# Gates computed as rows, cell products alternating between row halves, and value products of two key tiles in one run

## The reference

```python
# 1. the cell: q is the normalized x, k and v are the context; 4 heads of 64
igate, fgate = concat(q,k,v) @ ig_kernel + ig_bias, concat(q,k,v) @ fg_kernel + fg_bias   # 4 + 4 numbers a token
F = cumsum(log_sigmoid(fgate)); D = exp(F_s - F_t + igate_t - max)       # lower triangle, 512 x 512 a head
h = (q k^T / 8 * D) / normalizer @ v ; x = x + headnorm(h)
# 2. attention: 2 experts x 16 heads of 16 channels, on n1 = layernorm(x)
scores = q k^T / 4 ; attn = softmax(scores) ; ctx = attn @ v              # 32 heads, 512 x 512 each
x = x + sum over experts of (ctx @ wo + bo) * router
# 3. feed-forward: the best 2 of 8 experts of the batch, 256 -> 512 (gelu) -> 256
```

## Time and profile before

| | us |
|---|---|
| median of 3 runs (1590.46 to 1594.23) | 1592.3 |
| the profiled execution | 1590.36 |
| its span | 1588.7 |
| PE busy | 1455.0 (92%) |
| DVE busy | 1107.6 (70%) |
| ACT busy | 924.9 (58%) |
| POOL busy | 357.3 (22%) |
| mean granted TensorE clock | 0.954 |

### The profile page before, as it was taken

One profiled execution on the slowest core, in us unless ns is written; L12 is line 12 of the kernel. 1 busy time (PEld: TensorE's weight loads), 2 busy tenths in 40 slices (PEclk: granted clock), 3 DMA queues, 4 the chain that ended last, 5 costly groups with the idle time before them and its releaser, 6 DMA issues. The chain is left out here.

```text
span 1588.7 us, 22385 instructions
## 1 busy us (share of the span) xinstructions
PE 1455.0 (92%) x7724; PEld 733.8 (46%) x7724; DVE 1107.6 (70%) x2305; ACT 924.9 (58%) x1696; POOL 357.3 (22%) x342
## 2 busy tenths in 40 slices
PE   4358989999999999999999999999999999999977
PEld 4324433545445544545435444455435454444434
DVE  5537796787668866787568876788667876776531
ACT  1114756475666675575665765666664766657651
POOL 3321133122121223122131232212231221320100
PEclk9568989999999999999999999999999999999998
DMA  4064306431254306431163404532064211542001
GB/s 117 0 76 71 68 2 80 68 68 54 35 95 69 58 27 92 70 66 43 34 100 41 94 27 53 95 61 53 22 93 67 68 43 33 74 60 61 15 14 67
DMA packets 93793, 92.68 MB, mean 58 GB/s; under 512 B 16593, under 2 KB 88401, under 8 KB 92657
## 3 DMA queue, kind: packets, MB, share of 16 engines
q1 hardware_dynamic: 93680, 91.25, 33.1%
HBM read 36.10 MB, written 4.26 MB: 25 GB/s over the span
## 5 line engine op out<-in xcount | busy, mean ns | idle before, releaser
L1160 ACT ACTIVATE prob<-psum 128x512 f32<-128x512 f32 x1024 | 566.7, 601 | 332.7 <-PE psum L551 328.3
L945 DVE TENSOR_REDUCE mx<-psum 128x1 f32<-128x512 f32 x1024 | 645.0, 682 | 134.7 <-PE psum L536 133.9
L551 PE MATMUL psum<-qst,kst 98*128 98x512 bf16 x1024 | 358.2, 388 | 13.7 <-ACT cxT L1153 8.1
L536 PE MATMUL psum<-kst,qst 96*128 96x512 bf16 x1024 | 321.6, 392 | 25.9 <-issue 12.2
L566 PE MATMUL psum<-prob,vst 128*17 128x512 f32 x2048 | 274.9, 609 | 0.4 <-ACT prob L1160 0.2
L551 PEld LDWEIGHTS psum<-qst,kst 98*128 98x128 bf16 x1024 | 97.0, 100 | 261.9 <-issue 172.6
L536 PEld LDWEIGHTS psum<-kst,qst 96*128 96x128 bf16 x1024 | 101.0, 100 | 136.9 <-issue 25.2
L1262 POOL CAST parts<-resid 128x512 bf16<-128x512 f32 x64 | 39.5, 617 | 476.0 <-DVE resid L868 475.9
L526 PE MATMUL psum<-w,cxT 128*128 128x256 f32 x512 | 119.5, 380 | 5.2 <-ACT cxT L1153 5.2
L510 PE MATMUL psum<-n2T,x 128*128 128x512 f32 x256 | 117.5, 598 | 5.4 <-DMA x<-in_L_ffn_fw 5.4
L526 PEld LDWEIGHTS psum<-w,cxT 128*128 128x128 f32 x512 | 96.4, 190 | 25.4 <-issue 10.0
(11 more groups left out here) (176 smaller groups left out, 1733.1 us busy)
## 6 DMA issues: line engine op xcount, KB each, us to landing
kst<-parts SPq DMA_DIRECT2D x192, 128.0 KB, 4.5
qst<-parts SPq DMA_DIRECT2D x192, 128.0 KB, 5.4
cmat<-G_dram SPq DMA_DIRECT2D x8, 1024.0 KB, 4.9
x<-in_L_ffn_fw SPq DMA_DIRECT2D x16, 512.0 KB, 3.3
w<-in_L_ffn_fw SPq DMA_DIRECT2D x16, 512.0 KB, 3.9
kin<-in_ctx SPq DMA_DIRECT2D x8, 512.0 KB, 3.7
xbuf<-in_x SPq DMA_DIRECT2D x8, 512.0 KB, 4.6
out<-acc SPq DMA_DIRECT2D x8, 512.0 KB, 3.7
```

What stands on the lines that cost most here:

```text
L536: e.matmul(psum[:, u.bank, :], qst[0:KROWS, h, t * P:(t + 1) * P], kst[0:KROWS, h, :], start=True, stop=True).then_inc(u.full, 1)
L551: e.matmul(psum[:, u.bank, :], kst[0:KROWS + 2, h, g * P:(g + 1) * P], qst[0:KROWS + 2, h, :], start=True, stop=True).then_inc(u.full, 1)
L945: e.tensor_reduce(mx[:, qq * QUAD + j, t:t + 1], psum[:, u.bank, :], AX, ALU.max).then_inc(u.free, 1)
L1160: e.activation(prob[:, g % 2, j, :], psum[:, u.bank, :], ACT.Exp).then_inc(u.free, 1)
```

## The change

1. **Gates as rows.** The gate weights become the stationary operand, padded to 36 columns (forget gates at 0 to 3, input gates at 32 to 35), and the transposed tokens (512 wide) the moving one: 4 matmuls give both gates as rows. The copy by DVE and the 8 transposes are gone. The input gates come out at partitions 32 to 35, so a DMA moves them to 0 to 3 (`gi_moved`).
2. **Cell products alternate** between the row halves: two heads are taken together, block by block (`cd0`, `cd1` instead of `cd0` to `cd3`), into two banks; the cross products likewise.
3. **Value products of two key tiles in one run.** In the second slot of every other tile (slot % 8 == 1) stand the products of the two tiles before, 8 matmuls in one run: 128 runs.
4. **All slot tables and `AHEAD` are new.** Gelu pieces of ScalarE stand between exponentials in 7 places of a batch instead of 5; the program holds 116 ACT_TABLE_LOADs instead of 88.

```diff
-        wgate = sb("wgate", [P, 3 * KC, 2, NH])
-        wgkv = sb("wgkv", [P, KC, 2, NH])
-        gbias = sb("gbias", [NH, 2])
+        GI = 32
+        wgate = sb("wgate", [P, 2 * KC, GI + NH])
+        gbias = sb("gbias", [GI + NH, 1])
...
+        gi_made = cmat[GI:GI + NH, 0, :]
...
-        CARRY, MADE = QUAD - 1, 121
-        VALUES, COPY, TURN = 3, 3, 15
-        LATER, SENT = 1, 1
+        CARRY, MADE = QUAD - 1, 126
+        VALUES, COPY, TURN = 1, 5, 15
+        LATER, SENT = 1, 5
...
-                for t in range(NT):
-                    for c in range(2 * KC):
-                        src = (kT if c < KC else qT)[:, c % KC, t * P:(t + 1) * P]
-                        w_ = (wgkv if c < KC else wgate)[:, c % KC].rearrange("p g h -> p (g h)")
-                        ins = e.matmul(psum[:, u.bank, t * 2 * NH:(t + 1) * 2 * NH], src, w_, start=c == 0,
-                                       stop=c == 2 * KC - 1)
+                for c in range(2 * KC):
+                    src = (kT if c < KC else qT)[:, c % KC, :]
+                    ins = e.matmul(psum[0:GI + NH, u.bank, :], wgate[:, c, :], src, start=c == 0, stop=c == 2 * KC - 1)
                 ins.then_inc(u.full, 1)
-                gates = u
-
-                for g in (1, 0):
-                    yield f"grow{g}"
-                    u = take("grow", b, g)
-                    e.wait_ge(gates.free, gates.n)
-                    for t in range(NT):
-                        o = (t * 2 + g) * NH
-                        ins = transpose(psum[0:NH, u.bank, t * P:(t + 1) * P], gcol[:, o:o + NH], P)
-                    ins.then_inc(u.full, 1)
...
-                for h in range(NH):
-                    yield f"cd{h}"
-                    u = take("cd", b, h)
-                    o = DH * (h % 2)
+                for hp in range(NH // 2):
+                    yield f"cd{hp}"
+                    us = []
                     for c in range(NT):
-                        s_ = slice(c * P, (c + 1) * P)
-                        ins = e.matmul(psum[:, u.bank, s_], kT[o:o + DH, h // 2, s_], qT[o:o + DH, h // 2, s_],
-                                       start=True, stop=True)
-                    ins.then_inc(u.full, 1)
+                        for par in range(2):
+                            if c == 0:
+                                us.append(take("cd", b, 2 * hp + par))
+                            s_, half = slice(c * P, (c + 1) * P), slice(DH * par, DH * (par + 1))
+                            ins = e.matmul(psum[:, us[par].bank, s_], kT[half, hp, s_], qT[half, hp, s_], start=True,
+                                           stop=True)
...
-                            if j == VALUES:
-                                if g > 0:
-                                    values(b, qq, g - 1)
-                                elif qq > 0:
-                                    values(b, qq - 1, NT - 1)
+                            if slot >= 2 * QUAD and slot % (2 * QUAD) == VALUES:
+                                for n in (slot // QUAD // 2 * 2 - 2, slot // QUAD // 2 * 2 - 1):
+                                    values(b, n // NT, n % NT)
...
+                values(b, NQ - 1, NT - 2)
                 values(b, NQ - 1, NT - 1)
...
-                yield "gates"
-                u = uses["gates", b]
-                e.wait_ge(u.full, u.n)
-                e.tensor_copy(gcol, psum[:, u.bank, 0:2 * NG]).then_inc(u.free, 1)
...
+                yield "grow1"
+                u = uses["gates", b]
+                e.wait_ge(u.full, u.n)
+                e.activation(gf, psum[0:NH, u.bank, :], ACT.Identity, bias=gbias[0:NH, :]).then_inc(aa.here("gf"), 1)
+                yield "grow0"
+                e.activation(gi_made, psum[GI:GI + NH, u.bank, :], ACT.Identity, bias=gbias[GI:GI + NH, :]).then_inc(u.free, 1)
...
+                yield "gi"
+                u = uses["gates", b]
+                e.wait_ge(u.free, u.n)
+                e.dma_start(gi, gi_made).then_inc(gi_moved, 16)
```

More of the change, by code:

```diff
@@ L258, in build @@
[L258 to L269, removed]
+        CARRY, MADE = QUAD - 1, 126
+        VALUES, COPY, TURN = 1, 5, 15
+        LATER, SENT = 1, 5
+        PE_A = slots(4, "kT0:6 kT1:0 qT0:0 qT1:2 gates:15 cols:13 cd0 cd1:2 st0:0 st1:0 st2 num0:10 num1:5 num2 "
+                     "num3:24 n1T0:0 n1T1:3 p0:7 p1 p2:6 p3:2 pv0:24 pv1:0 logits")
@@ new lines, in build @@
+        ACT_S = slots(6, "p4:0 p5:16 p6:0 p7:9 v0:4 v1")
+        POOL_A = slots(-1, "pw:23 vcopy:13 mask0:2 mask1 mask2:25 mask3:0 vw:0 hw:13 hs:8 hn x2:29 r1:4 r5:2 s0:0 s1:0 "
+                       "s2:5 s3")
+        POOL_C = slots(30, "acc0:9 r1")
+        POOL_S = slots(13, "s4 s5:2 s6:21 s7")
+        SP_A = slots(4, "ctx:0 x:19 gi G:84 s0:0 s1:15 s2:0 s3")
+        SP_C = slots(53, "w10:10 w20:5 w11:0 w21:20 out")
+        SP_S = slots(9, "s4:0 s5:30 s6:0 s7")
+        AHEAD = ("2232001002134332000100400120220011223110000000101022111100411041"
+                 "0021014411101101102103121002020102110012030210020020120101000000")
@@ L424, in stage_a @@
                     ins.then_inc(u.full, 1)
-                    for par in range(2 if c else 0):
-                        u = take("cross", b, c, par)
-                        e.wait_ge(uses["st", b, c - 1].free, uses["st", b, c - 1].n)
-                        o = DH * par
-                        for hp in range(NH // 2):
-                            ins = e.matmul(psum[:, u.bank, hp * (DH + 1):(hp + 1) * (DH + 1)], qT[o:o + DH, hp, s_],
-                                           state[o:o + DH, c - 1, hp, :], start=True, stop=True)
-                        ins.then_inc(u.full, 1)
+                    us = []
+                    for hp in range(NH // 2 if c else 0):
+                        for par in range(2):
+                            half = slice(DH * par, DH * (par + 1))
+                            if hp == 0:
+                                us.append(take("cross", b, c, par))
+                                e.wait_ge(uses["st", b, c - 1].free, uses["st", b, c - 1].n)
+                            ins = e.matmul(psum[:, us[par].bank, hp * (DH + 1):(hp + 1) * (DH + 1)], qT[half, hp, s_],
+                                           state[half, c - 1, hp, :], start=True, stop=True)
+                            if hp == NH // 2 - 1:
+                                ins.then_inc(us[par].full, 1)
                 for c in range(KC):
@@ L651, in stage_a @@
                     set_ones(1)
[L653 to L656 removed]
                 yield "fa"
[L659 to L660 removed]
+                e.wait_ge(aa.sem, aa.at("gf", b))
                 e.scalar_tensor_tensor(out=ga, in0=gf, scalar=-1.0, in1=gf, op0=ALU.mult, op1=ALU.min
@@ L671, in stage_a @@
                 yield "g"
-                u = uses["grow", b, 0]
-                e.wait_ge(u.free, u.n)
+                e.wait_ge(gi_moved, 16 * (b + 1))
                 e.wait_ge(va.sem, va.at("F", b))
@@ L1042, in stage_a @@
                     e.activation(qT[:, c, :], psum[:, u.bank, :], ACT.Copy).then_inc(u.free, 1)
-                for g, dst in ((1, gf), (0, gi)):
-                    yield f"grow{g}"
-                    e.wait_ge(in_gates, 64)
-                    u = uses["grow", b, g]
-                    e.wait_ge(u.full, u.n)
-                    e.activation(dst, psum[0:NH, u.bank, :], ACT.Identity, bias=gbias[:, g:g + 1]).then_inc(u.free, 1)
+                yield "grow1"
[4 more added lines that the diff above has]
+                e.activation(gi_made, psum[GI:GI + NH, u.bank, :], ACT.Identity, bias=gbias[GI:GI + NH, :]).then_inc(u.free, 1)
                 yield "fa"
```

50 lines of the change are left out of this document (27 added, 23 removed), and 6 rows, old and new, of the table DVE_A.

## The result

The changed kernel takes 1552.0 us (median of 4 runs, 1549.32 to 1554.26), against 1592.6 us for the kernel before beside it (1590.46 to 1594.23). The ratio is 0.9745, 95% interval [0.9722, 0.9768]: 40.6 us faster. The forecast was 1529 us, so the gain was foretold as 63.2 us. The time lies inside the range, but a third of the gain is missing.

A forecast was written before the change was run, and what follows sets the result against it. TensorE bounds the kernel from first score to last; savings of 25.6, 6.3, 18.8, 12.3, 1.0 and 1.2 less 2.0 us sum to 63.2, so 1590.4 becomes 1527.2, median 1529 us; range 1511 to 1560 (2 in 10 left out).

The forecast's parts named there:

- Value products, 25.6: Value products on TensorE: 256 runs become 128, each saving 0.20 us of going into and out of 32-column positions: 25.6 us.
- Gates, the work, 6.3: Gates on TensorE: 8 instructions replace 32 plus 8 transposes, 0.9 us a batch in 7 batches: 6.3 us saved.
- Gates, the clock, 18.8: Half-clock stretches at the gates of 6 batches vanish with the 8-column matmuls: 18.8 us saved.
- Cell products, 12.3: Cell products: two heads side by side in alternating row halves, 1.75 us a batch in 7 batches: 12.3 us saved.
- the alternation gives nothing: Rival at the cell products: row halves take turns, 12.3 us less gain, 1541 us; chance 6%.
- cross products, 1.0: Three cross-product runs a batch, alternating row halves: 1 us saved in all, since most of it overlaps already.
- Start, 1.2: Before the first score: the first gate row reaches ScalarE at 22.5 instead of 23.69 us, 1.2 us saved.
- New order, waits, -2.0: TensorE's waits under the new slot order, at gelus and near slot 120: +0.3 us a batch, 2 us lost.
- (a): Second tile needs the exponential two slots back, next tile's first exponential waits for the run; 0.5 us a batch lost.
- ScalarE becomes the bound in the gelu stretches: Rival: two more gelu visits and one slot-120 wait stop TensorE, 4.05 us a batch, 1557 us; chance 14%.
- The clock falls at the gates all the same: Rival: something else in the gates' slots causes the half clock, 18.8 us less gain, 1548 us; chance 8%.
- Slower, the second tile waits for its exponentials: Rival at the value runs: TensorE waits for the second tile's exponentials, 0.7 us a run gives 1611 us; chance 3%.

The follow-up runs named there:

- the early-read run: Kernel before with only the gates as rows, old slot tables, ScalarE reading both gate rows in slot 12: 1575.4 us, ratio 0.9890.
- the first run: Kernel before with only the gates as rows, old slot tables, ScalarE's two reads in slots 14 and 15: 1590.5 us, ratio 0.9984.

## Why the prediction was right, and where it was not

**TensorE sets the time: right.** Most of the signs that the prediction named are there: 128 runs of 1.84 us to the next score, gates of 3.6, cell runs of 1.12, no half clock at the gates. The batch takes 176.7 us instead of 175, and its waits are 6.9 us, not near 5.

**Value products, 25.6: right in size.** The price of the arrangement was read well. One run of the changed kernel:

```profile
853.39 0.38 PE L528 MATMUL psum<-kst,qst 96*128 96x512 bf16 x1
853.70 1.91 PE L558 MATMUL psum<-prob,vst 128*17 128x512 f32 x16
855.54 0.39 PE L543 MATMUL psum<-qst,kst 98*128 98x512 bf16 x1
```

1.84 us to the next score, 0.31 from the product ahead to the run instead of 0.22. Over a full batch at full clock the runs' starts give 29.57 us instead of 31.50, and 11 fewer entries behind a score or maximum product save 0.9 more: 2.85 a batch, 0.18 a run, 22.8 us in all. What was wrong was to book this as time saved: as built on the old tables the same pairs lose 114 us, and 23 with the hold removed.

**Gates, the work, 6.3: right in the starts** (0.76 a batch instead of 0.9: 8 instructions pace 3.56 us; going into them takes 0.31 us instead of 0.22, half of the 0.2 that the working allowed for the 36 columns). In the run with the gates alone, read early, it didn't reach the batch. **Gates, the clock, 18.8: right**, and the place too. With the 8-column matmuls gone and no wait in their place, no stretch of half clock stands at the gates (run with the early read). The new form differs in more than its columns (8 weight loads instead of 32, no transposes), so which trait the clock answers to isn't shown. Over the six full batches the clock gave back 22.2 us, since of the three stretches behind the gelu's waits only one is left; the early-read run, which keeps the old gelu order, has five.

**Cell products, 12.3: right in the starts.** 16 instructions of two heads:

```profile
861.72 1.19 PE L386 MATMUL psum<-qT,kT 64*128 64x128 f32 x16
862.84 0.39 PE L543 MATMUL psum<-qst,kst 98*128 98x512 bf16 x1
```

1.12 us to the score, nearly like one head alone in the earlier trace rows (1.08). 1.61 us a batch were saved in the pace (1.75 foretold); alone, the part gave 8.9 us. The rival "the alternation gives nothing" is out for the cell products. For the **cross products, 1.0**, it is right: with the old tables a run of 8 takes 0.59 us alternating and 0.60 before, 0.01 us a batch in all. The 0.2 us a batch that the changed kernel shows (0.14 foretold) come from the third run alone, which takes 0.59 in its new place instead of 0.78; alternating alone, on the old tables, left it there (0.79). So the number was right by luck.

**Start, 1.2: right.** The gate row stands at 22.48 on ScalarE, as against 23.69 in the earlier trace rows; the first score gained 1.0:

```profile
22.48 0.68 ACT L1036 ACTIVATE cmat<-psum,gbias 4x512 f32<-4x512 f32 x1 [6.69 <-PE psum L353]
```

**New order, waits, -2.0: this step failed.** At the gelus the sum of the waits was near, the waits themselves mostly others. ScalarE, then TensorE:

```profile
919.86 2.06 ACT L1149 ACTIVATE prob<-psum 128x512 f32<-128x512 f32 x4
...
923.24 0.60 ACT L1142 ACTIVATE cxT<-psum 128x512 f32<-128x512 f32 x1
...
925.14 0.60 ACT L1149 ACTIVATE prob<-psum 128x512 f32<-128x512 f32 x1
...
927.05 0.60 ACT L1142 ACTIVATE cxT<-psum 128x512 f32<-128x512 f32 x1
...
928.96 2.06 ACT L1149 ACTIVATE prob<-psum 128x512 f32<-128x512 f32 x4
```

```profile
919.42 0.38 PE L543 MATMUL psum<-qst,kst 98*128 98x512 bf16 x1
920.51 0.39 PE L543 MATMUL psum<-qst,kst 98*128 98x512 bf16 x1 [0.71 <-ACT prob L1149]
...
923.88 0.65 PE L311 MATMUL psum<-ident,ctxs 128*128 128x128 f32 x4 [0.78 <-ACT cxT L1142]
...
927.93 0.38 PE L543 MATMUL psum<-qst,kst 98*128 98x512 bf16 x1
929.62 0.39 PE L528 MATMUL psum<-kst,qst 96*128 96x512 bf16 x1 [1.30 <-ACT prob L1149]
```

0.71 + 0.78 + 1.30 = 2.8 us where 2.4 stood in the working. The last is the one foretold for the bank of score 80 (1.6): its exponential is the first of the four from 928.96. The other one foretold, 0.8 for exponential 79 (925.14), didn't come. Instead TensorE had waited twice before: 0.71 behind the second gelu, for the bank of exponential 75 (the first from 919.86), and 0.78 for the third gelu's own reading (923.24). That the sums agree is luck. The 0.5 us near slot 120 didn't come either.

The step priced the order as +0.3 us a batch. What is lost there is 3.7: 2.2 of idle time, and 1.5 in the pace of scores and maximum products once the entries saved are taken out. (Shorter transposes and the like gave about 0.8 back, which I hadn't foretold.) Not all of this is shown to be the new order's: gates and cell products on the old tables lost 1.5 a batch in the same two ways, 0.7 and 0.8. The sum had no term for that. Three things were missed.

1. *I priced the waits that I looked for and took the others as unchanged.* In a full batch TensorE's waits of 1.2 (the row `<- issue`) and for `qbuf` (0.7) are new, and neither came up in the working. The first is probably one for the transfer `qst<-parts`, for which the program lets the first maximum product of a quad wait: TensorE goes on with ScalarE, which that transfer held. ScalarE's hold isn't new (3.1 before); TensorE's is.

```profile
958.68 0.38 PE L528 MATMUL psum<-kst,qst 96*128 96x512 bf16 x1 [1.15 <-issue]
958.70 0.69 ACT L1107 ACTIVATE parts<-psum,bqs 128x512 bf16<-128x512 f32 x1 [2.74 <-DMA qst<-parts]
```

2. *A wait costs more than its idle time.* The score at 919.42 ends at 919.80 and the next starts at 920.51: 1.09 us from start to start instead of 0.22, for a wait of 0.71. The overlap, 0.16, is lost too.
3. *The last batch was counted as an eighth of the rest.* Its slots are 1.17 us long (149.3 by 128) instead of 1.38, because `stage_a` is absent. Distances written in slots are shorter in time there, and the idle time rose from 3.6 to 11.6 us: 8 of the 27 us that the profiled execution lacks. It rose with singles on the new tables to 6.5, with pairs and three buffers on the old ones to 8.8, so both seem to share in it. Neither the third buffer nor the sixth visit took it away (10.1 to 11.0). That the shorter slots are its cause is argued, not shown.

Two costs of the order were shown by removing them: a gelu visit less gave 9 us, the hold 10 to 14 (1.5 to 2.6 of it before the first score, where those kernels load less). The larger part of the second I had before me: the prediction asked of the pairs only whether the *value products* would wait for exponentials (they don't, 2.1 us), not whether *exponentials* would wait for the value products. The sentence "the first exponential of the tile after waits for the first half of the run" stood in (a) and was then not priced. The range for this step (-30) just covers the outcome, -29 if all that is missing is booked here.

The Trainium skill, "TensorEngine Tiling (Array Packing)", section "Performance Considerations", warns that the emptying of PSUM may become the bottleneck when tiling speeds up TensorE. The traces agree only in part: ScalarE, which empties the score banks, became late (253.8 us of held exponentials with pairs alone), yet for want of a buffer to write and not of throughput, since it is busy 54% in that run (62% in the changed kernel).

**The rivals.** "ScalarE becomes the bound in the gelu stretches" (1557) comes nearest to the measured time, and its price, 4.05 us a batch in waits, is close to the 3.7 found. But it put all of it at the gelus and near slot 120. The gelus hold 2.8 us, near slot 120 next to nothing stands; the rest is elsewhere. "The clock falls at the gates all the same" came true only in part and only with the late read: 3.41 us in five batches of the first run. "Slower, the second tile waits for its exponentials" named the wrong direction of the wait. In the other direction it came true on the old tables: 1685 us, some of it the late read.

**Still open.** Which pieces of the new tables bring the 40 us that they are worth with three buffers. Why single tiles on the new tables are as slow as 1612.8 us. Why the clock falls behind the gelu's waits in three full batches of the kernel before, in five with the early read and in one of the changed kernel, though the waits are of like size in each batch: a wait alone doesn't decide it. Why the scores pace slower when other work of TensorE shrinks. What a third buffer does for the kernel before with single tiles, which would show that it has no other use. Moving the copy of the projections so that the wait for `qst<-parts` goes wasn't tried.

## What to carry to other kernels

When work is merged into longer runs, ask for each buffer that the run reads who will *write* it next and how much stands ahead of the run: two buffers with runs of two tiles leave the writer no slack, and here that was 93 of 114 us lost on the old order and some 10 on the new. Work taken from a busy engine isn't yet time: at full clock gates and cell products saved 2.4 us a batch in their own starts and 0.9 in the batch. Price a new order by the waits in every stretch, the lightest batch by itself, and add the lost overlap to each wait. And test a part of a change together with the order that it needs: singly, the pairs lost 114 us, the gates gained almost nothing with a read one slot late and 16 us with it early.

## What the runs showed of the hardware

- TensorE's granted clock can stay at its higher level (1.00, 2.4 GHz) for 887 us on end with 7.3 to 8.1 us of idle time per 177 us batch, waits of 1.3 us among it. In the kernel before and in the early-read run it fell to 0.50 (1.2 GHz) for 3.41 us after waits of the same size, in some batches.
- Runs of matmuls with 8 moving columns were followed by half clock while TensorE was busy throughout. With 512 columns (and 8 weight loads instead of 32) for the same result, and no wait, it wasn't.
- A 64-row float32 matmul of 128 columns in one row half and one in the other start 0.03 us apart or less; 16 of them take 1.12 us to the next score, 8 in one half 1.08.
- Going into the arrangement in 32-column positions costs 0.09 us (0.31 from start to start instead of 0.22), whether 8 or 16 instructions follow. Going into matmuls with 36 columns of weights costs the same.
